# All of g(s) on VectorE: the last 128 columns taken off GpSimd in a causal polynomial attention

## The reference

```
att = (q . k) / sqrt(64), masked to -inf above the diagonal
att = polymax(att)             # x > 0: (x*x + 1)/1000;  -100 <= x <= 0: (1 - 0.01*x)/1000;  masked: 0
y   = att @ v                  # no normalization over a row
x   = x + y @ W_proj
x   = x + gelu(LN(x) @ U1 @ V1 + b1) @ U2 @ V2 + b2
```

## Time and profile before

| | us |
|---|---|
| median of three runs | 2625.9 (2624.9 to 2629.9) |
| the profiled execution, its own time | 2639.3 |
| its span on core 1, the slowest | 2637.8 |
| spans of cores 0 to 3 | 2635.2 to 2637.8 |
| spans of cores 4 to 7 | 2612.6 to 2623.6 |
| busy on core 1: PE, DVE, POOL, ACT | 1417.5, 1296.5, 1059.9, 774.9 |

### The profile page before, as it was taken

How to read it: one execution, slowest core, us unless ns; L and a number is a source line. 1 busy time by engine, 2 the same in 40 slices (tenths; PEclk the granted TensorE clock), 3 DMA queues, 4 the chain that set the end, 5 groups by cost and what they waited for, 6 DMA issues and landing times.

```text
span 2637.8 us, 25581 instructions; the slowest of 8 cores (2612.6 to 2637.8 us)
## 1 busy us (share of the span) xinstructions
PE 1417.5 (54%) x6880; PEld 486.5 (18%) x6880; DVE 1296.5 (49%) x2171; ACT 774.9 (29%) x1074; POOL 1059.9 (40%) x1028
## 2 busy tenths in 40 slices
PE   3423875855555545444444535665555528137886
PEld 0101332421111111111111112331111103002332
DVE  4584322477666645444444422348766643334332
ACT  1100000055555544444444400015555520013333
POOL 0000000055777788888888800015677730000000
PEclk7655777955555555555555568985555558558888
DMA  5353011000000000000000021000000014400001
GB/s 163 121 184 109 31 33 64 1 1 1 1 1 1 1 1 0 0 1 0 1 1 0 1 64 56 9 1 1 1 1 1 1 48 160 143 0 1 32 32 64
DMA packets 37420, 87.88 MB, mean 33 GB/s; under 512 B 1953, under 2 KB 7330, under 8 KB 37282
## 3 DMA queue, kind: packets, MB, share of 16 engines
q1 hardware_dynamic: 30562, 75.75, 8.5%
q10 hardware_dynamic: 6720, 10.49, 1.3%
HBM read 77.85 MB, written 8.39 MB: 33 GB/s over the span
## 4 chain that ended last, share of the span: by engine, by line
POOL 38%; PE 30%; DVE 9%; DMA 8%; issue 8%; ACT 5%; POOLq 0%; DVEq 0%; SPq 0%; ACTq 0%
POOL poolD L733 20%; POOL poolD L738 18%; DMA poolD<-W_attn 4%; ACT poolD L711 3%; PE ps L690 3%; PE ps L614 3%; PE ps L594 3%; PE ps L1060 3%; PE ps L883 2%; PE ps L868 2%; PE ps L974 2%; PE ps L636 2%; PE ps L1080 2%; PE ps L772 1%; DMA poolD<-W_proj 1%
## 5 line engine op out<-in xcount | busy, mean ns | idle before, releaser
L733 POOL TENSOR_SCALAR poolD<-poolD 128x256 bf16<-128x256 bf16 x512 | 600.3, 1172 | 1038.9 <-ACT poolD L716 862.6
L711 ACT ACTIVATE poolD<-ps 128x1024 bf16<-128x1024 f32 (+3 forms) x640 | 566.5, 896 | 1365.0 <-PE ps L690 677.3
L725 DVE SCALAR_TENSOR_TENSOR poolD<-poolD 128x768 bf16<-128x768 bf16 (+2 forms) x640 | 619.9, 974 | 454.4 <-ACT poolD L711 317.6
L772 PE MATMUL ps<-poolD,poolA 128*64 128x512 bf16 (+3 forms) x1280 | 363.8, 557 | 636.5 <-POOL poolD L738 566.7
L738 POOL TENSOR_TENSOR poolD<-poolD 128x256 bf16<-128x256 bf16 x512 | 459.4, 897 | 42.8
L690 PE MATMUL ps<-poolB,poolA 64*128 64x512 bf16 (+3 forms) x1280 | 329.8, 541 | 34.3 <-ACT poolD L711 16.7
L772 PEld LDWEIGHTS ps<-poolD,poolA 128*64 128x64 bf16 x1280 | 101.7, 130 | 873.4 <-issue 868.7
L1072 ACT ACTIVATE poolC<-ps,sb_b1s 128x512 bf16<-128x512 f32 x128 | 87.5, 687 | 124.9 <-PE ps L1060 81.3
L716 ACT ACTIVATE poolD<-ps,consts 128x256 bf16<-128x256 f32 x256 | 120.6, 471 | 0.0
L690 PEld LDWEIGHTS ps<-poolB,poolA 64*128 64x128 bf16 x1280 | 67.2, 105 | 283.1 <-issue 281.9
L746 DVE TENSOR_TENSOR poolD<-poolD,sb_masksb 128x256 bf16<-128x256 bf16 x256 | 118.2, 462 | 0.0
(11 more groups left out here) (102 smaller groups left out, 1180.9 us busy)
## 6 DMA issues: line engine op xcount, KB each, us to landing
poolD<-x_t SPq DMA_DIRECT2D x8, 2048.0 KB, 9.4
poolA<-x_t SPq DMA_DIRECT2D x8, 2048.0 KB, 9.2
poolD<-W_attn SPq DMA_DIRECT2D x12, 1024.0 KB, 4.9
poolD<-W_attn SPq DMA_DIRECT2D x16, 512.0 KB, 3.6
poolC<-x_own_t SPq DMA_DIRECT2D x8, 1024.0 KB, 5.0
y<-poolC SPq DMA_DIRECT2D x4, 2048.0 KB, 6.6
poolD<-W_proj SPq DMA_DIRECT2D x8, 512.0 KB, 3.9
poolD<-U ACTq DMA_DIRECT2D x5, 512.0 KB, 4.5
```

What stands on the lines that cost most here:

```text
L711: e.activation(o, i, AF.Relu), inc="S")
L725: e.scalar_tensor_tensor(o, i, 0.01, i, ALU.add, ALU.mult),
L733: e.tensor_scalar_add(o, i, 0.01), inc="P", ss=True)
L772: e.matmul(o, l, r, skip_group_check=True, start=st, stop=True, tile_position=tp),
```

## The change

The split of g between DVE and POOL is taken out. L725's instruction (L724 in the changed kernel) covers all N columns of both heads. POOL's two instructions and their waits are gone, `pcnt` is always 0, so that AV waits for no POOL, and `e_relP` stays 0, so that ACT waits for none.

```
-                        hi = N - 128 if N >= 384 else N
                         gcnt[idx] = b.op("vector",
-                                         lambda e, o=gb[:, 2 * sb:2 * sb + 2, 0:hi],
-                                         i=eb[:, 2 * sb:2 * sb + 2, 0:hi]:
+                                         lambda e, o=gb[:, 2 * sb:2 * sb + 2, 0:N],
+                                         i=eb[:, 2 * sb:2 * sb + 2, 0:N]:
                                          e.scalar_tensor_tensor(o, i, 0.01, i,
                                                                 ALU.add, ALU.mult),
                                          inc="V")
-                        if hi < N:
-                            b.wait("gpsimd", "S", s_rel[sb])
-                            b.wait("gpsimd", "T", g_rel[sb])
-                            b.op("gpsimd", lambda e, o=abh[:, :, :],
-                                 i=eb[:, 2 * sb:2 * sb + 2, hi:N]:
-                                 e.tensor_scalar_add(o, i, 0.01), inc="P", ss=True)
-                            pcnt[idx] = b.op("gpsimd",
-                                             lambda e, o=gb[:, 2 * sb:2 * sb + 2, hi:N],
-                                             a=abh[:, :, :],
-                                             i=eb[:, 2 * sb:2 * sb + 2, hi:N]:
-                                             e.tensor_mul(o, a, i), inc="P", ss=True)
-                            e_relP[sb] = pcnt[idx]
-                        else:
-                            pcnt[idx] = 0
+                        pcnt[idx] = 0
```

## The result

The changed kernel takes 2117.9 us in the median against 2625.8 before. The ratio is 0.806, with a 95% interval of 0.8055 to 0.8072. 508 us are gone; I had forecast 490, and a time of 2136. The profiled execution took 2121.2 us, its span on core 5, the slowest, 2119.7. Two executions, 2148 and 2188 us, in which the cores of one die ran at a lower clock, are outside the ratio.

A forecast was written before the change was run, and what follows sets the result against it. POOL in attention was taken as the bound, 2.23 us a k-tile; attention would fall from 1372 to 882 us (passes 865, tails 16, lead-in about 1), saving 490 and giving 2136 us; range 2095 to 2205.

The forecast's parts named there:

- the ring: Attention before the change: POOL, ACT, DVE wait in turn; POOL alone never waits, at 2.23 us a k-tile.
- 1024 columns take DVE 1.23 us, and start every 1.15: DVE's g on unmasked k-tiles after the change: 1.23 us long, less 0.08 overlap, so 1.15 us start to start.
- the 0.96 us for 768 columns: DVE's g before the change, read as having no POOL beside it; with 0.27 more it gave 1.23 us.
- The overlap of 0.08 between DVE instructions: In attention, DVE's next waiting instruction starts 0.08 us before the last ends, also across a semaphore wait.
- rival 3: No overlap on DVE in attention: 0.08 us more for each L725 and mask, 92 us, 2228 us; chance 0.05.
- DVE is late, with 0.04 us to spare over PE at half clock: Unmasked k-tiles after the change: DVE's 1.15 us is the new bound, against PE's 1.11 at half clock.
- rival 1: PE at half clock sets the pace on unmasked k-tiles, 1.25 us: 38 us lost, 2174 us; chance 0.19.
- The boundary: Between attention passes: all PE and ACT, it stays; 3.91 us from a full pass's last g to the next first g.
- Rival 2: Clock rises in attention: boundaries save 20 us, perhaps the 16 us of tail too, DVE still the bound; 2100 us; chance 0.12.
- The allowance of 16 us for tails: Ends of 32 masked passes: 0.50 us each added because k-tiles are too narrow for DVE alone to set the time.
- the full passes: Sixteen attention passes, forecast at 21.16 us each after the change: 15 x 1.15 + 3.91.
- the short ones: Sixteen attention passes of masked k-tiles, forecast at 12.03 us each before the allowance: 8.96 + 3.07.

The follow-up runs named there:

- The two halves: pool_unmasked and pool_masked: each undoes the change on one kind of k-tile of the changed kernel; 2542.6 and 2211.3 us.
- pool_64: Kernel before, with POOL's share halved to 64 columns of each head and DVE doing the other 448; 2406.6 us.
- g_768: Changed kernel, but DVE leaves out the last 128 columns of each head where N is at least 384, and nobody does them; 2039.4 us.
- pool_unmasked: Kernel before, with POOL's share given to DVE on masked k-tiles only; POOL keeps it on the 384 unmasked ones; 2542.6 us.
- pool_masked: Kernel before, with DVE doing all of g on unmasked k-tiles; POOL keeps its share on the 128 masked ones with N of 512 and 384; 2211.3 us.
- pool_beside: Changed kernel, plus POOL's two old instructions on its own data on every second k-tile with N of 384 or 512, nobody waiting; 2293.6 us.

## Why the prediction was right

Step by step, as it was put:

- *POOL is the member of the ring that never waits.* In the kernel before POOL has no gap above 0.1 us within a full pass. The two halves show that the gain lies in the k-tiles with a share of POOL's, and pool_64 that with half the share the pass follows POOL again. How much of POOL's 2.23 us is its own work and how much DVE beside it, no run separates. With 0.85 and 0.67 us and two gaps it would be 1.68 (an estimate), still more than DVE's 1.13.
- *1024 columns take DVE 1.23 us, and start every 1.15.* 1.22 and 1.13. One premise was misread: the 0.96 us for 768 columns was taken as one with no POOL beside it, but in the earlier trace rows it starts at 1203.67, while POOL's L733 still runs (to 1203.90), and L738 follows. The number holds all the same: g_768, with no POOL, has 0.96 us in the mean. The overlap of 0.08 between DVE instructions holds with a semaphore wait between; rival 3 falls. The Trainium skill, "VectorE: DVE Perf Modes", section "The DRAIN you can't avoid", would have it that the pipe empties first; here the exception that it allows is the rule.
- *DVE is late, with 0.04 us to spare over PE at half clock.* PE's 1.11 us were exact, as g_768 showed. In the changed kernel DVE has no idle time inside a full pass, so rival 1 fell.
- *The boundary.* 3.91 us were forecast from the last g of a full pass to the next; it is 3.85 in 12 of 15 cases. From QK to ACT it is now 0.79 (907.50 to 908.29, in the time line below), where 0.84 passed in the earlier trace rows. At these boundaries it is 0.84 or 0.85 in before, pool_unmasked and pool_64, where ACT also waits for POOL, and 0.79 in the changed kernel, pool_masked and pool_beside, where it doesn't (but for one boundary each in pool_unmasked and pool_masked). The further wait seems to cost about 0.05 us.

```profile
908.29 1.94 ACT L711 ACTIVATE poolD<-ps 128x1024 bf16<-128x1024 f32 x2 [3.79 <-DVE poolC L807]
```

- *Rival 2, a higher clock in attention.* It came true in part: 0.68 and 0.60 against 0.50. It is worth almost nothing, since DVE sets the pace, and at 12 of the 15 boundaries AV still took 0.60 to 0.61 us, as at half clock. Only 3 were shorter, by 0.1 to 0.24 us.
- *The allowance of 16 us for tails* is the step that failed. This was a term of the sum with a wrong cause. I took the tail's length of 2.18 us for a property of narrow k-tiles, "where POOL no longer plays a part". It was POOL's part: pool_masked has it, pool_unmasked has not. The changed kernel's tail takes 1.68 us, to the digit what my own steps gave. It does so at half clock (AV on 256 columns takes 0.42 us in it, as in the earlier trace rows), so rival 2, which let the tail go with a higher clock, didn't come true there either. Without the allowance the saving would have been 506 us, against 508 measured.

In sum: 882 us were forecast for attention, 862 were measured; 16 of the 20 are the allowance, and 5 the full passes (16 x 0.31), less 1 for the short ones.

## What to carry to other kernels

Before work is shared between VectorE and GpSimd, price the helper by its full effect. Here its 256 columns saved DVE 0.27 us. The helper itself became the slowest member of the ring, with its instructions stretched by DVE's (1.17 and 0.90 us in the mean, 0.85 and 0.67 at the shortest), and even where nobody waited for it the pair cost DVE 0.64 us. When an engine leaves the path, don't carry over a delay seen near it: follow the waits of that stretch back by as many steps as there are buffers. A sum that meets the total may still have the wrong bound: compare it kind by kind, as pool_64 shows. And once one engine is relieved, list the next ones with their price per tile (DVE 1.13, PE 1.11 at half clock, ACT 0.92 us without a bias operand here); that list tells what a further step can bring.

## What the hardware showed that I had not expected

- A POOL instruction with no tie to DVE made the attention passes 0.32 us longer. A quarter of a microsecond, read off one pair of rows, was too little.
- Halving POOL's columns from 256 to 128 took only 0.24 and 0.19 us off its two instructions in the mean (from 1.17 and 0.90), while the shortest of each fell by 0.32 and 0.24 (from 0.85 and 0.67).
- A bias operand read from SBUF makes ACT's relu on 1024 columns 1.14 us instead of 1.02 to 1.05.
- A product of a bf16 tile with itself takes 0.69 us on 1024 columns, the scalar_tensor_tensor 1.22.
